# Gated cross-attention with routed experts: the setup rebuilt, with keys and values placed by transfers inside SBUF, clearing on GpSimd, double-buffered queries, and expert weights fetched along the attention loop

## The reference

```python
def attention(q_in, k_in, v_in, mask, Wq, bq, Wk, bk, Wv, bv, Wo, bo):   # 16 heads of 16
    q, k, v = heads(q_in @ Wq + bq), heads(k_in @ Wk + bk), heads(v_in @ Wv + bv)
    score = where(mask, -1e30, einsum('bhqd,bhkd->bhqk', q, k) / sqrt(16))
    return heads_joined(softmax(score) @ v) @ Wo + bo

def ffn(x, ...):                        # 8 experts of width 1024, the 2 best of each row, one shared
    combine = renormalised top 2 of softmax(x @ gate_w.T)
    y = gelu(x @ W1[e] + b1[e]) @ W2[e] + b2[e]
    return sum_e(y * combine) + gelu(x @ sW1 + sb1) @ sW2 + sb2

x = x + tanh(g_xattn) * attention(layernorm(x), ctx, ctx, mask, ...)
x = x + tanh(g_ffn) * ffn(layernorm(x), ...)
```

## Time and profile before

| | us |
|---|---|
| median of 3 runs (lowest, highest) | 609.38 (598.23, 610.87) |
| the profiled execution | 600.51 |
| its span in the profile | 598.9 |
| TensorE busy in it | 538.7 (90%) |
| VectorE busy | 380.0 (63%) |
| ScalarE busy | 240.2 (40%) |
| GpSimd busy | 224.4 (37%) |

### The profile page before, as it was taken

The page is one execution under the profiler, slowest core; times in us unless marked ns, Lnnn a source line. Parts: engine busy times, 40 slices in busy tenths (PEclk is TensorE's granted clock), DMA queues, the critical chain, the costliest instruction groups (busy, mean ns, idle before and its releaser), DMA issues.

```text
span 598.9 us, 12255 instructions
## 1 busy us (share of the span) xinstructions
PE 538.7 (90%) x3223; PEld 467.9 (78%) x3224; DVE 380.0 (63%) x787; ACT 240.2 (40%) x528; POOL 224.4 (37%) x194
## 2 busy tenths in 40 slices
PE   2815968999999869999999999999999999999995
PEld 2615958888888758887888888888888888888884
DVE  7405555888787557766666555655565555655888
ACT  1300234666766443343343434334343434334331
POOL 4106525511100004772534444435444444301773
PEclk9975587989999879999999999999999999999999
DMA  7689295453337332335647674755665665311454
GB/s 239 218 214 254 85 275 149 130 149 105 96 101 241 124 114 72 123 108 164 177 139 237 197 231 125 239 145 172 197 231 156 235 187 195 98 35 51 138 171 122
DMA packets 74358, 96.45 MB, mean 161 GB/s; under 512 B 6125, under 2 KB 61661, under 8 KB 74341
## 3 DMA queue, kind: packets, MB, share of 16 engines
q0 software_dynamic: 23712, 57.18, 31.3%
q1 hardware_dynamic: 44181, 33.94, 19.0%
q10 hardware_dynamic: 6448, 5.12, 2.6%
HBM read 70.04 MB, written 21.97 MB: 154 GB/s over the span
## 4 chain that ended last, share of the span: by engine, by line
PE 62%; POOL 10%; DVE 10%; issue 8%; ACT 5%; DMA 5%; SPq 0%; POOLq 0%; DVEq 0%; ACTq 0%
PE ps L632 13%; PE ps L619 7%; PE ps L620 7%; PE ps L621 7%; PE ps L633 7%; PE ps L607 6%; POOL gath L551 5%; POOL routed_x L515 5%; PE ps L702 3%; PE ps L673 3%; PE ps L646 2%; DMA moved_q<-xT 2%; PE ps L600 2%; PE ps L688 2%; DVE xT L1099 1%
## 5 line engine op out<-in xcount | busy, mean ns | idle before, releaser
L632 PE MATMUL ps<-w2hl,hTh 128*128 (+1 forms) x440 | 162.4, 408 | 2.9 <-DVE hTl L1163 2.9
L633 PE MATMUL ps<-w2hl,hTl 128*128 (+1 forms) x440 | 123.7, 281 | 0.0
L995 ACT ACTIVATE hid<-hid 128x512 f32<-128x512 f32 x110 | 69.2, 632 | 132.2 <-DVE hid L1169 132.2
L632 PEld LDWEIGHTS ps<-w2hl,hTh 128*128 128x128 f32 x440 | 82.9, 188 | 21.4 <-issue 3.7
L989 ACT ACTIVATE hTh<-ps 128x512 fp32r<-128x512 f32 x110 | 60.0, 597 | 95.1 <-PE ps L607 95.1
L1169 DVE TENSOR_TENSOR hid<-ps,b1bc 128x512 f32<-128x512 f32 x110 | 75.3, 689 | 30.2 <-PE ps L621 25.4
L619 PE MATMUL ps<-w1l,xT 128*128 (+1 forms) x220 | 92.6, 421 | 0.0
L620 PE MATMUL ps<-w1h,xT 128*128 (+1 forms) x220 | 87.6, 398 | 0.0
L621 PE MATMUL ps<-w1h,xT 128*128 (+1 forms) x220 | 87.2, 396 | 0.0
L633 PEld LDWEIGHTS ps<-w2hl,hTl 128*128 128x128 f32 x440 | 82.9, 188 | 0.0
L1163 DVE TENSOR_TENSOR hTl<-ps,hTh 128x512 fp32r<-128x512 f32 x110 | 70.8, 685 | 0.0
(11 more groups left out here) (166 smaller groups left out, 797.3 us busy)
## 6 DMA issues: line engine op xcount, KB each, us to landing
stage<-in_L_ffn_W POOLq DMA_DIRECT2D x16, 1024.0 KB, 6.3
w1h<-in_L_ffn_W POOLq DMA_DIRECT2D x8, 1024.0 KB, 6.8
w2hl<-in_L_ffn_W POOLq DMA_DIRECT2D x8, 1024.0 KB, 8.0
qstack<-moved_q SPq DMA_DIRECT2D x48, 128.0 KB, 2.4
xrow<-routed_x SPq DMA_DIRECT2D x39, 128.0 KB, 2.3
routed_y<-yrow ACTq DMA_DIRECT2D x39, 128.0 KB, 1.7
routed_x<-zeros SPq DMA_DIRECT2D x6, 768.0 KB, 3.9
stage<-in_L_ffn_sW POOLq DMA_DIRECT2D x4, 1024.0 KB, 6.3
```

What stands on the lines that cost most here:

```text
L632: mm(p_y, hTh[:, c, :], part(2 * D), start=c == 0, stop=False)
L633: last = mm(p_y[:, 0:D], hTl[:, c, :], part(D), start=False, stop=c == FC - 1)
L995: act.activation(hid[:, n, :], hid[:, n, :], ACT.Gelu).then_inc(S["h_act"], 1)
```

## The change

Keys: instead of one write to HBM and three reads back, twelve transfers inside SBUF copy four groups of 32 partitions into each of three bands of `kstack`, eight on SP's queue and four on ScalarE's. Values: the matmuls with copies of the identity (`spread`) and the masked copies out (`spread_out`) go; 25 transfers inside SBUF copy pieces of `vals` of 1 to 77 partitions into `spread_v`, which has been cleared, 15 on SP's queue and 10 on ScalarE's. The layouts of both are turned so that a row of a piece is one run of 544 bytes. Clearing `kstack` and `spread_v` and setting `qstack` to one is done by three whole memsets on GpSimd, where VectorE did parts of it; the masks for pairs of heads go with their 20 instructions. Queries: qT becomes a double buffer in `hid`, and the order on SP becomes keys, queries 0 and 1, values, queries 2 to 4. The order of TensorE and VectorE in setup puts all values before the third queries and the statistics of the later tiles. Context and weights of setup lie in the weight staging tiles, so the first staging transfer waits for the last value matmul; the weight transfers and the two pairs of subtractions are spread between the `key_diag`s of all batches.

```diff
+    SEGMENTS = []
+    for j, (h0, h1, at, n) in enumerate(CHUNKS):
+        for h in range(h0, h1):
+            key0, key1 = max(h * SK, j * P), min(h * SK + SK, j * P + n)
+            SEGMENTS.append((j, at + h - h0, h, key0 - h * SK, key0 - j * P, key1 - key0))
...
-            "k (b h d) -> k b h d", b=B, d=DH + 1)
-        copies = hid[:].rearrange("p n f -> p (n f)")[0:SK, 0:3 * SK].rearrange("k (o q) -> k o q", o=3)
-        pairmask = a("pairmask", [P, NPAIR])
-
-        spread_v = a("spread_v", [P, B, NPAIR, DH + 1])
-
-        early = spread_v[:].rearrange("p b n d -> p (b n d)")
+            "k (h b d) -> k h b d", b=B, d=DH + 1)
+
+        spread_v = a("spread_v", [P, NPAIR, B, DH + 1])
+
+        early = stage1[:].rearrange("p c f -> p (c f)")
         ctxT = early[:, 0:C * CTX].rearrange("p (c n) -> p c n", c=C)
-        wk, wv = (early[:, C * CTX + n * C * D:C * CTX + (n + 1) * C * D].rearrange("p (c n) -> p c n", c=C)
-                  for n in range(2))
+        wk = early[:, C * CTX:C * CTX + C * D].rearrange("p (c n) -> p c n", c=C)
+        wv = stage2[:, 0:C, :]
...
-        qT = xT
+        qT = hid[:].rearrange("p u (s c q) -> p u s c q", s=2, c=C)
...
+        def qrow(t, part, c):
+            return qT[:, bass.ds(t % 2, 1), part, c, :].rearrange("p o q -> p (o q)")
+
+        def stacked(row, g):
+            return kstack[row * ROWS:(row + 1) * ROWS].bitcast(F32).rearrange("r (c g) n -> r c g n", c=C)[:, :, g, :]
+
+        def keys_of(part, g):
+            return kT[g * ROWS:(g + 1) * ROWS, part, :, :].bitcast(F32)
...
             def move_keys():
-                sp.wait_ge(S["kT_lo"], 2 * C)
-                sp.dma_start(k_moved_to.rearrange("s c p n -> p s c n"), kT.bitcast(F32)).then_inc(S["k_moved"], 16)
-                sp.wait_ge(S["k_moved"], 16)
-                for row, part in enumerate((0, 1, 0)):
-                    sp.dma_start(kstack[row * ROWS:(row + 1) * ROWS, :, :].bitcast(F32),
-                                 k_moved_to[part].rearrange("c (g r) n -> r (c g) n", r=ROWS)
-                                 ).then_inc(S["k_stacked"], 16)
+                sp.wait_ge(S["k_zero"], 1)
+                for row, part in ((0, 0), (1, 1)):
+                    sp.wait_ge(*((S["kT_sb"], 2 * C) if part == 0 else (S["kT_lo"], 2 * C)))
+                    for g in range(P // ROWS):
+                        sp.dma_start(stacked(row, g), keys_of(part, g)).then_inc(S["k_stacked"], 16)
+
+            def spread_values():
+                sp.wait_ge(S["v_zero"], 1)
+                sp.wait_ge(S["v_sb"], B // 2)
+                for j, pair, h, key, to, n in SEGMENTS:
+                    if j >= SPREAD_ACT:
+                        sp.dma_start(spread_v[to:to + n, pair, :, :], vals[key:key + n, h, :, :]).then_inc(S["v_spread"], 16)
...
-                sp.dma_start(there.rearrange("s c p q -> p s c q"), qT[:].bitcast(F32)).then_inc(S["q_moved"], 16)
+                sp.dma_start(there.rearrange("s c p q -> p s c q"), qT[:, parity]).then_inc(S["q_moved"], 16)
...
+            move_keys()
+            sp.wait_ge(S["ones_set"], 1)
             move_queries(0, 0)
-            move_keys()
-            for t in range(1, AHEAD):
+            move_queries(1, 1)
+            spread_values()
+            for t in range(2, AHEAD):
...
+            pool.memset(headsel[:], MASKED).then_inc(S["consts"], 1)
...
-            for j, (h0, h1, pair, _) in enumerate(CHUNKS):
-                m = pairmask[:, pair:pair + h1 - h0]
-                ge = pool.affine_select(out=m, in_=m, compare_op=ALU.is_ge, fill=0.0, base=j * P - h0 * SK,
-                                        pattern=[[-SK, h1 - h0]], channel_multiplier=1)
-            ge.then_inc(S["consts"], 1)
...
+            pool.memset(kstack[:].bitcast(F32), 0.0).then_inc(S["k_zero"], 1)
+            pool.memset(qstack[:].bitcast(F32), 1.0).then_inc(S["ones_set"], 1)
+            pool.memset(spread_v[:], 0.0).then_inc(S["v_zero"], 1)
+            pool.wait_ge(S["k_zero"], 1)
...
-            pool.wait_ge(S["consts"], 14)
-            pool.wait_ge(S["x_in1"], 16)
-            load_w1(0, sW1_v)
-            load_w2(0, sW2_v)
...
+            pool.wait_ge(S["sel_set"], 1)
+            pool.wait_ge(S["k_stacked"], 16 * 2 * (P // ROWS))
+            pool.wait_ge(S["k_stacked_act"], 16 * (P // ROWS))
             key_diag(0)
+            key_diag(1)
+            pool.wait_ge(S["x_in1"], 16)
+            pool.wait_ge(S["v_ps"], B // 2)
             load_b1(0, shared_b[0])
             load_b2(0, shared_b[1])
+            load_w1(0, sW1_v)
+            key_diag(2)
             load_hi1(0, sW1_v)
+            load_w2(0, sW2_v)
+            key_diag(3)
             load_hi2(0, sW2_v)
-            key_diag(1)
             split_w1(0, 0)
+            ready_1(0)
+            key_diag(4)
             load_w1(1, expert_w1(0))
-            ready_1(0)
-            key_diag(2)
             split_w2(0, 0)
+            ready_2(0)
+            key_diag(5)
             load_w2(1, expert_w2(0))
-            ready_2(0)
             load_b1(1, expert_b(0)[0])
             load_b2(1, expert_b(0)[1])
             load_hi1(1, expert_w1(0))
+            key_diag(6)
             load_hi2(1, expert_w2(0))
-            key_diag(3)
             split_w1(1, 1)
+            key_diag(7)
             load_w1(2, expert_w1(1))
             ready_1(1)
-            key_diag(4)
             split_w2(1, 1)
             load_w2(2, expert_w2(1))
             ready_2(1)
-            for b in range(5, B):
-                key_diag(b)
...
-                    pe.wait_ge(S["v_spread"], 2)
-                    spread(4)
-                    spread(5)
...
+                    if known and t == 0:
+                        pe.wait_ge(S["v_spread_act"], 16 * sum(seg[0] < SPREAD_ACT for seg in SEGMENTS))
+                        pe.wait_ge(S["v_spread"], 16 * sum(seg[0] >= SPREAD_ACT for seg in SEGMENTS))
...
+            norm_in(0, p_in)
             pe.wait_ge(S["wv_in"], 16)
             values((0, 1))
-            norm_in(0, p_in)
             pe.wait_ge(S["wq_in"], 16)
             queries(0)
-            pe.wait_ge(S["kT_lo"], 2 * C)
             values((2, 3))
             pe.wait_ge(S["q_sb"], 1)
             norm_in(1, p_in)
+            values((4, 5))
             queries(1)
-            values((4, 5))
+            pe.wait_ge(S["kT_lo"], 2 * C)
+            values((6, 7))
             pe.wait_ge(S["q_sb"], 2)
             norm_in(2, p_in)
             queries(2)
-            values((6, 7))
             pe.wait_ge(S["v_sb"], B // 2)
-            pe.wait_ge(S["copies_set"], 1)
-            for q in range(2):
-                spread(q)
+            pe.wait_ge(S["ones_set"], 1)
             scores(0, 0)
-            for q in range(2, 4):
-                spread(q)
...
+                if not isinstance(t, int) or t >= 2:
+                    act.wait_ge(S["q_moved"], 16 * (t - 1))
...
+            act.wait_ge(S["k_zero"], 1)
+            for g in range(P // ROWS):
+                act.dma_start(stacked(2, g), keys_of(0, g)).then_inc(S["k_stacked_act"], 16)
...
+            act.wait_ge(S["v_zero"], 1)
+            act.wait_ge(S["v_sb"], B // 2)
+            for j, pair, h, key, to, n in SEGMENTS:
+                if j < SPREAD_ACT:
+                    act.dma_start(spread_v[to:to + n, pair, :, :], vals[key:key + n, h, :, :]
+                                  ).then_inc(S["v_spread_act"], 16)
...
-            dve.memset(vals[:], 1.0).then_inc(S["mask_set"], 1)
-            dve.memset(qstack[ONE:ONE + 1, :, :, :].bitcast(F32), 1.0).then_inc(S["mask_set"], 1)
-            dve.memset(kstack[ONE:P].bitcast(F32), 0.0).then_inc(S["mask_set"], 1)
+            dve.memset(vals[:, :, :, DH:DH + 1], 1.0)
             dve.wait_ge(S["consts"], 8)
             ts(iota_far[:], iota_i[:], -FAR, None, ALU.add).then_inc(S["far_set"], 1)
-            dve.tensor_copy(copies, ident[0:SK, 0:SK].unsqueeze(1).to_broadcast([SK, 3, SK])
-                            ).then_inc(S["copies_set"], 1)
...
-                for q in {0: (4, 5), 1: (6,), 2: (7,)}.get(t, ()) if isinstance(t, int) else ():
-                    spread_out(q)
...
+            values(0)
             queries_lo(0)
             norm_in(1)
-            values(0)
             values(1)
             queries_lo(1)
             norm_in(2)
+            values(2)
+            values(3)
+            queries_lo(2)
             dve.wait_ge(S["x_in1"], 16)
-            statistics(FIRST, NT // 2)
-            values(2)
-            queries_lo(2)
-            statistics(NT // 2, NT)
+            statistics(FIRST, NT)
...
-            dve.wait_ge(S["consts"], 14)
-            for q in range(4):
-                spread_out(q)
```

74 lines of the change are left out of this document (13 added, 61 removed).

## The result

The changed kernel took 598.42 us as the median of 12 runs (592.66 to 608.97), the kernel before 605.76 as the median of 12 runs beside it (598.23 to 613.12). The ratio is 0.9878, with a 95% interval of 0.9831 to 0.9925: 1.2% faster, well inside the 2% that I had called "no change". The forecast was 578 us, and 597 was the top of the range. The profiled executions are 600.51 and 592.66 us (spans 598.9 and 591.0), a ratio of 0.987, about that of the medians. Both lie near the fast end of their kernel's runs.

What follows compares the result with a forecast made beforehand. It took setup to wait on SP's queue moving keys and queries, with TensorE filling the untouched feed-forward part. -24.7 - 2.2 - 5.8 + 4.7 + 1 (clock) = -27.0 from 600.5 gives 573.5, plus 4.5 makes 578 us; range 564 to 597.

Steps and rivals of the forecast that it cites:

- term 4: Weight loads moved into the loop cost +4.7 us; GpSimd's own order of key_diags and subtractions costs nothing.
- The burst that I took at 3.6: Loop: 2.6 MB of loads issued together behind key_diag(5), priced at 0.9 to 6.2 us, taken at 3.6.
- Term 1: Setup: the scores of tile 1, released by VectorE's subtraction, start at 41.8 instead of 66.54, a gain of 24.7 us.
- The values: Setup: 25 issues at 0.45 us, 6.8 us on SP and 4.5 on ScalarE, landing in time, costed at nothing.
- Terms 2 and 3: Loop: no spread matmuls before the scores of tile 2, -2.2 us; smaller hole before those of tile 3, -5.8 us.
- Loads hidden: Loop: the double buffer and earlier query moves give slack, so weight loads cost nothing: 570 us, chance 0.13.
- Placement late: Setup: value pieces spread over too few engines, or keys at half rate, lose ten to fourteen us: 590 us, chance 0.16.
- The slower rival: Loop: each of nine 1 MB loads delays a query move by 8.3 us, 5.9 beyond slack: 618 to 623 us, chance 0.04.
- The slow clearing: Setup: GpSimd clears at 1.8 ns an element, delaying the first value copy and queries about 8 us: 586 us, chance 0.1.
- My 4.5 us between the profiled execution and the median: Whole time: 4.5 us added to the sum of 573.5, midway between two groups of executions, giving 578.

Runs made afterwards that it cites:

- e1: Changed kernel with GpSimd's key_diags 3 to 7 and the four weight subtractions waiting until x2row of the step is written: 589.63 us, 0.9788.
- e12: As e9, with key_diags 3 and up also waiting for a norm of the step: 596.48 us, 0.9826 of the kernel before.
- e9: Changed kernel with all weight loads and subtractions of phases 0 and 1 issued only after the scores of tile 14: 607.82 us, 1.0055.
- e2: Changed kernel with GpSimd's order of weights, key_diags and subtractions put back to that of the kernel before: 605.43 us, 0.9979.
- e13: Changed kernel with the query buffer number a constant instead of t % 2 in a register, loops over pairs of steps: 587.13 us, 0.9703.
- e15: Changed kernel with the constant buffer number of e13 and the GpSimd waits of e1: 586.36 us, 0.9727.
- e3: Changed kernel with the first weight load and two biases issued after key_diag(2) instead of before it: 603.86 us, 1.0002.
- e14: As e7, but each weight load is released by the landing of a query move instead of by a norm: 586.62 us, 0.9653.
- e7: Changed kernel with norm-released key_diags and one load a step, value pieces early on ScalarE, and a constant buffer number: 588.94 us, 0.9739.
- e16: As e14 without the early value pieces on ScalarE: 589.17 us, 0.9706.
- e11: As e12 with the constant buffer number and value pieces issued early on ScalarE: 591.46 us, 0.9807.
- e4: Changed kernel with all 25 value pieces issued on SP's queue, none on ScalarE's: 603.83 us, 0.9927.

## Why the prediction was wrong, by its steps

The direction was right and the size was not: 27 us forecast, 7.9 measured in the profiled executions and 7.3 between the medians.

**The step that failed** is this sentence of term 4: "Each key_diag keeps about two steps of cover and each subtraction follows one whose data came long before, so GpSimd's order itself costs nothing". I asked only who waits for GpSimd's results. Nobody does, as forecast. But GpSimd and VectorE stop each other while they work, and VectorE's norms stand on TensorE's path. In the kernel before four x2row had been held too, to 0.96 to 1.68 us, and no xn by a key_diag; in the changed kernel two xn and one x2row stood for the length of a GpSimd operation. e1 and e12 take that away by timing alone and get 7.1 and 8.6 us of the ten steps back, 4.2 and 9.4 us at first up. This is shown, best by e12 against e9. That e2, with the old order, is held too says that the list of loads did not set up the held xn; e13 says that the register did. The x2row of 4.50 us fell under a weight subtraction, whose moment the new order set; no run takes that one apart.

**A cost I had not listed** is the double buffer's computed number. The prediction puts it at nothing and never names it. The operands of queries and queries_lo are addressed by t % 2 at run time, and the low part starts 0.26 us later behind the high one, which also brought xn under key_diag. The runs with a constant number are 5 to 7 us quicker over ten steps. Between e1 and e15, where nothing is held in either, it is 5.2: 2.4 of it is nine times 0.26 to 0.27, and where the rest comes from stays open. The edit also halves the number of turns of the two loops, and no run tells the two apart. TensorE's waits for xn fall along with it, from 4.1 us in e1 to 1.6 in e15.

**Term 4's own sum held, in part by luck.** +4.7 us were forecast for the loads in the loop; the ten steps show 4.5 (after against e9) to 7.3. The burst that I took at 3.6 shows as a hole of 4.92 us in e1. In the changed kernel the wait on the queries is 1.3 us in all: the burst was issued from 108.84 to 111.6, and in the step lengthened by a held xn no query move was issued between 104.92 and 116.63. So its 4.5 us come from other steps than the forecast had them in.

**Term 1** was forecast at 24.7 and gave 20.2. Its reasoning up to the subtraction was right to 1 us: it ended at 40.8 in the changed kernel, and e3 and e9, which have no early weights, start the scores of tile 1 at 41.66 and 41.88, released by the subtraction as forecast, against 41.8. What failed is that I let the first weights delay the values and not queries 1, which were moved at 30.98 and stacked from 34.42 beside them (issued at 34.58). Clearing took 8.9 us for a forecast of 8.3, and key_diag(0) started at 29.07 for a forecast of about 28.

**The values** were put at 0.45 us an issue and "6.8 us", from SP's rows of whole moves. They took 12.05. With that "queries 2 are then stacked at 41.5 + 2.7 + 1.3 + 2.4 = 47.9" fell: the move started only at 47.98. That is a part of why tile 2 is at 59.6 and tile 3 at 68.88, not at about 61; the other part is weights again, since e9, where the move starts as late (48.97) and no weights are about, has tile 2 at 56.32 and tile 3 at 64.85. Terms 2 and 3 are there (no spread matmuls, and no hole of 7.11 us before tile 3), but up to tile 4 the three terms together gave 23.1 where 24.7 + 2.2 + 5.8 - 1 = 31.7 were forecast, 8.6 too few; 4.0 of these are early weights, by e9's tile 4 at 73.52. The ten steps then took 16.8 more where 4.7 were forecast, 12.1 too many. 27.0 - 8.6 - 12.1 = 6.3, the measured lead at first up.

**The rivals.** Loads hidden is out: they cost 4.5 us or more. Placement late had its chance with the queries and not with the values: the product of tile 0 with the values starts at 50.97 and never waits on a transfer, so no run here tests what that rival was built on, how many engines a piece is spread over. The slower rival named the right mechanism, a move that takes 10.6 us behind a weight load, and e1 has one of 10.5, but only one and not nine. The slow clearing did not come. My 4.5 us between the profiled execution and the median was 5.8.

**How much was there to win.** The best versions are e13, e14 and e15, 0.9703, 0.9653 and 0.9727 with overlapping intervals: about three per cent instead of 1.2. All five kernels at 0.974 or below (e7 and e13 to e16) have the constant number and loads in the loop; with the number in a register none came under 0.9788. No run came to the forecast 573.5 / 600.5 = 0.955. What the setup wins is partly given back by the loads, which in every order tried either met the queries, ahead of tile 1 (after), of tile 2 (e3), at 120 to 131 us (e1, e15), or came too late behind tile 14 (e9, e11).

## What to carry to other kernels

An engine whose results nobody waits for can still be on the path, if the two can stop each other, as these two did: put its long operations where the other has none that it can hold, and look for instructions whose duration in the timeline is a multiple of their own minimum. Ask of any small delay what it moves next to what: a lead of 0.4 us had kept the kernel before clear, and 0.26 us more in one engine's chain nearly used it up. Price a stop of TensorE with the slow clock that follows it. When setup gets shorter, ask at once where the loads that lay there go now, and time both ends of the loop: a gain at tile 4 says little about first up.

## What the runs showed of the hardware

- A tensor_scalar of VectorE (128x256, 0.41 us alone) that starts 0.03 to 0.09 us before, or at any time during, a GpSimd tensor_tensor ends 0.13 to 0.17 us after that one: 2.42 to 2.47 us beside 2.24 (14 times), 4.48 to 4.50 beside 4.51 to 4.53 (4 times). One that starts 0.12 to 0.24 us before is free, and GpSimd's takes 2.30 to 2.42. With 0.35 us or more between the starts (e13, the kernel before) neither is longer.
- An operand addressed by a register instead of a constant put the low part of a query 0.92 to 0.95 us behind the high part instead of 0.66, in one and the same trace (changed kernel).
- A stop of 2.1 us by such a hold cost 2.9 us of the ten steps on the mean in e9 against e12; in the changed kernel two holds in one step, 2.53 and 3.60 us of waiting, made it 16.9 us long instead of 8.5; TensorE's clock was 0.50, 1.2 GHz, from 132 to 140 us, although it worked without a pause from 136.
- A transfer from SBUF to SBUF of one piece of the values held its queue for 0.80 us on SP, alone (20.06 for 25, e4) or beside ScalarE's (12.05 for 15), and 0.86 on ScalarE (8.64 for 10); the whole moves of the earlier trace rows took 0.38 to 0.45, one of them 0.76.
- A query move of 256 KB, 2.3 us alone, took 10.5 us when it was issued amid 2.6 MB of weights and biases (e1), and the three reads into qstack beside the first 1.6 MB up to 11 (changed kernel).
